# First cross attention of a two-layer perceiver: 16 rounds of one head become 32 rounds of half a head's keys, with a running maximum

## The reference, cut to what matters

```python
N_HEADS = 16
bs, width, length = qkv.shape            # 1, 256, 512
ch = width // N_HEADS                     # 16
q = qkv.reshape(bs * N_HEADS, ch, length)
k = v = y.reshape(bs * N_HEADS, ch, -1)   # 16 heads, 16 channels, 8192 keys
scale = 1.0 / math.sqrt(math.sqrt(ch))
weight = jnp.einsum('bct,bcs->bts', q * scale, k * scale)
weight = jax.nn.softmax(weight.astype(jnp.float32), axis=-1)
a = jnp.einsum('bts,bcs->bct', weight, v)
```

## Time and profile before

| | |
|---|---|
| median of 3 runs | 1461.67 us (1461.64 to 1463.94) |
| the profiled execution, its time | 1462.05 us |
| its span, first to last instruction | 1460.3 us |
| PE busy over the span | 1395.1 us, 96% |
| DVE busy | 1158.6 us, 79% |
| ACT busy | 938.6 us, 64% |
| POOL busy | 107.5 us, 7% |
| the first cross attention in the span | 0 to 705.8 us |

### The profile page before, as it was taken

How to read it: one execution, slowest core, us unless ns; L and a number is a source line. 1 busy time by engine, 2 the same in 40 slices (tenths; PEclk the granted TensorE clock), 3 DMA queues, 4 the chain that set the end, 5 groups by cost and what they waited for, 6 DMA issues and landing times. The chain is left out here.

```text
span 1460.3 us, 27039 instructions
## 1 busy us (share of the span) xinstructions
PE 1395.1 (96%) x10692; PEld 848.0 (58%) x10692; DVE 1158.6 (79%) x1638; ACT 938.6 (64%) x1738; POOL 107.5 (7%) x98
## 2 busy tenths in 40 slices
PE   3999999999999999999899999999989889999998
PEld 1533333333333333333357899999978664567998
DVE  5999999999999999993577666666658546887665
ACT  1188888888888888889275445455534541785553
POOL 8301111111110111100000000000000000000000
PEclk9999999999999999999999999999999999999999
DMA  7334465544544444455203654554446523104540
GB/s 171 85 71 101 115 163 143 143 132 101 115 88 113 91 96 100 115 74 73 87 1 136 266 191 172 186 200 174 173 151 267 230 81 151 65 2 159 190 177 38
DMA packets 36191, 189.34 MB, mean 130 GB/s; under 512 B 8904, under 2 KB 9328, under 8 KB 24048
## 3 DMA queue, kind: packets, MB, share of 16 engines
q1 hardware_dynamic: 35888, 187.62, 42.9%
q10 hardware_dynamic: 192, 0.20, 0.1%
HBM read 163.23 MB, written 21.27 MB: 126 GB/s over the span
## 5 line engine op out<-in xcount | busy, mean ns | idle before, releaser
L451 DVE TENSOR_REDUCE pm<-bank 128x1 f32<-128x1024 f32 x512 | 621.6, 1222 | 18.6 <-PE bank L525 15.7
L505 ACT ACTIVATE probs<-bank 128x512 f32<-128x512 f32 x1024 | 553.6, 598 | 122.5 <-PE bank L540 60.3
L525 PE MATMUL bank<-kst,qst 50*128 50x512 f32 x1024 | 371.7, 460 | 27.2 <-DMA qst<-qsplit 20.5
L540 PE MATMUL bank<-qst,kst 50*128 50x512 f32 x1024 | 363.0, 445 | 2.0 <-DVE pm L451 0.8
L553 PE MATMUL bank<-probs,vext 128*32 128x256 f32 x3840 | 306.5, 391 | 0.0
L540 PEld LDWEIGHTS bank<-qst,kst 50*128 50x128 f32 x1024 | 150.0, 184 | 213.7 <-ACT probs L505 195.5
L1200 PE MATMUL bank<-e_xhi,e_hi 128*128 128x256 f32 (+1 forms) x784 | 222.3, 284 | 3.2 <-DVE e_lo L1135 2.6
L1200 PE MATMUL bank<-e_xhi,e_lo 128*128 128x256 f32 (+1 forms) x784 | 222.2, 283 | 0.0
L1200 PE MATMUL bank<-e_xlo,e_hi 128*128 128x256 f32 (+1 forms) x784 | 222.1, 283 | 0.0
L525 PEld LDWEIGHTS bank<-kst,qst 50*128 50x128 f32 x1024 | 148.2, 189 | 46.1 <-DVE pm L451 23.8
L553 PEld LDWEIGHTS bank<-probs,vext 128*32 128x32 f32 x3840 | 75.6, 108 | 170.8 <-issue 94.2
(11 more groups left out here) (218 smaller groups left out, 1496.9 us busy)
## 6 DMA issues: line engine op xcount, KB each, us to landing
raw<-wall SPq DMA_DIRECT2D x34, 1536.0 KB, 6.6
kst<-kscratch SPq DMA_DIRECT2D x192, 128.0 KB, 4.3
raw<-wall SPq DMA_DIRECT2D x10, 2304.0 KB, 8.6
kscratch<-ksplit SPq DMA_DIRECT2D x15, 1024.0 KB, 4.5
kraw<-ctx_rows SPq DMA_DIRECT2D x16, 512.0 KB, 4.3
vraw<-ctx_vt SPq DMA_DIRECT2D x16, 512.0 KB, 4.7
ctxT<-ctxT SPq DMA_DIRECT2D x8, 1024.0 KB, 12.2
nat<-ctx_chunks SPq DMA_DIRECT2D x6, 1024.0 KB, 21.5
```

The lines of the kernel that those rows point to most:

```text
L451: nc.vector.tensor_reduce(pm[:, h % 2, r % 4, r // 4:r // 4 + 1], bank[:, 2 * (r % 2):2 * (r % 2) + 2, :], AX.XY, ALU.max).then_inc(pre_re ...
L505: nc.scalar.activation(probs[:, (XT * h + n) % PR, :], bank[:, bank_of(h, n), :], ACT.Exp, scale=XSCALE).then_inc(probs_ready, 1)
L525: ins = nc.tensor.matmul(bank[:, 2 * (r % 2) + j, :], qst[64 * j:64 * j + KR, h, tt * P:tt * P + P], kst[64 * j:64 * j + KR, h % 2, c * 51 ...
L540: nc.tensor.matmul(bank[:, bank_of(h, n), :], kst[64 * j:64 * j + KR, h % 2, m * P:m * P + P], qst[64 * j:64 * j + KR, h, :], start=True, ...
```

## The change

A head's 8192 keys are taken in two halves, and the loop's unit is now half a head (`k`, 32 of them; h, half = divmod(k, 2)), with 16 rounds, 32 scores and 8 value groups each. The first half is exponentiated against its own maximum, the second against the maximum over the whole head (a running maximum in `pm`). Two more rows of `qst` (50 and 51) hold the second half's negated maximum; in `kst`, rows 48 and 49 hold ones for the first half of the keys and zeros for the second, rows 50 and 51 hold ones. These rows are written from a small tile `marks` with four transfers instead of POOL's memsets.

The maxima go through memory: one transfer writes `nblocks` to `nscratch`, SP waits for it, and two read it back into `qst`. This is now done for every half head.

The first half's sums have to be multiplied by the exponential of the difference of the maxima: POOL takes the difference (`mdiff`), ACT the exponential (`weight`), SP sends it through memory to all partitions (`store_weight`, `spread_weight`), POOL multiplies (`weigh`) and adds the halves (`sum_o`). ACT copies bank 6 to `osb` twice a head, after the seventh exponential of a unit (`n == 6`).

The first value group of a unit is now whole (`pv_group`) and stands at the end of round 11. `FIRST_BUSY` goes from 18 to 4: idle-filling matmuls begin in round 4 of the first unit's 16 rounds, formerly in round 18 of 32. The order of SP's transfers and of POOL's work is rewritten. In the last unit, PE sums head 15's two halves in bank 2 and 3 with matmuls.

```diff
-KR = 3 * XC + 2
+KR = 3 * XC
+NS = 2
+XN = NS * XH
-XP = XT // 2
-XG = XT // 4
+XST = XT // NS
+XP = XST // 2
+XG = XST // 4
-LAST_BANKS = [0, 1, 4, 5, 7]
+LAST_BANKS = [0, 1, 7, 4, 5]
-FIRST_BUSY = 18
+FIRST_BUSY = 4
...
+            def stack_negmax(k):
+
+                sp.wait_ge(negmax_turned, k + 1)
+                sp.dma_start(nscratch[k], nblocks[:, k % 2, :]).then_inc(negmax_stacked, 16)
+                sp.wait_ge(negmax_stacked, 64 + 48 * k + 16)
+                for j in range(2):
+                    row = 64 * j + KR + 2 * (k % NS)
+                    sp.dma_start(qst[row:row + 2, k // NS, :].rearrange("k (t q c) -> k t q c", t=4, q=4).bitcast(F32),
+                                 nscratch[k].rearrange("(q k t) c -> k t q c", q=4, k=8)[0:2]).then_inc(negmax_stacked, 16)
+
+            def store_weight(h):
+
+                sp.wait_ge(weight_ready, h + 1)
+                sp.dma_start(wscratch[h].rearrange("(p t) -> p t", t=4), weight[:, :]).then_inc(weight_moved, 16)
+
+            def spread_weight(h):
+
+                sp.wait_ge(weight_moved, 32 * h + 16)
+                if h > 0:
+                    sp.wait_ge(weighted, h)
+                sp.dma_start(weights[:, :, :].rearrange("p c t -> p (c t)"), wscratch[h].partition_broadcast(P)).then_inc(weight_moved, 16)
...
-            def stack_negmax(h):
-
-                sp.wait_ge(negmax_turned, h + 1)
-                for j in range(2):
-                    for q in range(4):
-                        to = qst[64 * j + 32:64 * j + 34, h, :].rearrange("k (t q c) -> k t q c", t=4, q=4)[:, :, q, :]
-                        sp.dma_start(to.bitcast(F32), nblocks[32 * q:32 * q + 8, h % 2, :]).then_inc(negmax_stacked, 16)
...
+            def weigh(h):
+
+                pool.wait_ge(weight_moved, 32 * h + 32)
+                pool.wait_ge(o_copied, NS * h + 1)
+                first = osb[:, 0, :].rearrange("p (t c) -> p c t", t=4)
+                nc.gpsimd.tensor_tensor(first, first, weights[:, :, :], ALU.mult).then_inc(weighted, 1)
+
+            def sum_o(h):
+
+                pool.wait_ge(weighted, h + 1)
+                pool.wait_ge(o_copied, NS * h + 2)
+                nc.gpsimd.tensor_tensor(osb[:, 1 + h % 2, :], osb[:, 1 + h % 2, :], osb[:, 0, :], ALU.add).then_inc(o_summed, 1)
...
-                    if n == 5 and h > 0:
-                        copy_o(h - 1)
-            copy_o(XH - 1)
+                    if n == 6 and k > 0:
+                        copy_o(k - 1)
+                    if n == 26 and k % NS == 0:
+                        act.wait_ge(apart, k // NS + 1)
+                        if k // NS > 0:
+                            act.wait_ge(weight_moved, 32 * (k // NS))
+                        nc.scalar.activation(weight[:, :], mdiff[:, k // NS % 2, :], ACT.Exp, scale=XSCALE).then_inc(weight_ready, 1)
+            copy_o(XN - 1)
...
-            for h in range(XH - 1):
+            for k in range(XN - 1):
                 for i in range(XP):
                     for e in range(2):
-                        late_score(h, 2 * i + e)
-                        pre(h + 1, i, 1 - e)
-                        if e == 0 and i == FIRST_V + 1:
-                            late_values(h, FIRST_V)
-                    if h == 0 and i < LAGP:
-                        first_busy(3, 1)
-                    elif h == 0 and i < LAGP + 1 + PVLAG:
+                        late_score(k, 2 * i + e)
+                        pre(k + 1, i, 1 - e)
+                    if k == 0 and i < LAGP:
+                        first_busy(3)
+                    elif k == 0 and i < FIRST_V:
                         for n in range(2):
-                            nc.tensor.matmul(bank[:, 6, :], qst[0:KR, 1, 0:P], kst[0:KR, 1, 0:512], start=True, stop=True)
-                    if i != FIRST_V:
-                        late_values(h, i)
+                            nc.tensor.matmul(bank[:, 6, :], qst[0:KR, 0, 0:P], kst[0:KR, 0, 0:512], start=True, stop=True)
+                    if i == FIRST_V + 1:
+                        pv_group(k, 0)
+                    elif i != FIRST_V:
+                        late_values(k, i)
```

More of the change, by code:

```diff
@@ L357, in _ @@
             load_nd(XH - 2)
-            sp.wait_ge(scores, XT * (XH - 1))
+            sp.wait_ge(scores, XST * (XN - 2))
             for h in range(XHA):
@@ L363, in _ @@
         def _(pool):
-            for j in range(2):
-                nc.gpsimd.memset(qst[64 * j + 32:64 * j + 34, 0, :].bitcast(F32), 0.0).then_inc(const_set, 1)
-            pool.wait_ge(const_set, 2)
             nc.gpsimd.memset(ident[:, :], 0.0).then_inc(g.ident_ready, 1)
@@ L372, in _ @@
             pool.wait_ge(g.ident_ready, 2)
-            for j in range(2):
-                nc.gpsimd.memset(kst[64 * j + 32:64 * j + 34, 0, 0:XK // 2].bitcast(F32), 1.0).then_inc(const_set, 1)
-            pool.wait_ge(const_set, 4)
             def split(h):
@@ L428, in _ @@
+            weigh(XH - 1)
         @block.vector
@@ L543, in pv, with values_ready @@
-            def pv(h, q, half):
+                        pe.wait_ge(probs_ready, XST * k + n + 1 - len(LAST_BANKS))
+                elif k > 0 or n >= 3:
+                    pe.wait_ge(probs_ready, XST * k + n - 2)
+                nc.tensor.matmul(bank[:, bank_of(k, n), :], kst[64 * j:64 * j + rows, h % 2, m * P:m * P + P],
+                                 qst[64 * j:64 * j + rows, h, :], start=True, stop=True).then_inc(scores, 1)
+            def values_ready(k, q):
+                pe.wait_ge(probs_ready, XST * k + 4 * q + 4)
+                if q == 0:
+                    if k % NS == 0:
+                        pe.wait_ge(v_ready, k // NS + 1)
+                    if k > 0:
+                        pe.wait_ge(o_copied, k)
```

264 lines of the change are left out of this document (143 added, 121 removed).

## The result

The changed kernel takes 1467.97 us (median of 6 runs, 1466.2 to 1471.51), the kernel before 1461.66 (6 runs, 1460.74 to 1463.94): ratio 1.0042, 95% interval 1.0032 to 1.0053. It is 6.3 us slower, where 4.3 us faster was forecast. The profiled execution took 1468.59 us.

A forecast was written before the change was run, and what follows sets the result against it. PE's rounds bound the steady pace (1.233 us), with a stall per head and a chain of reads at the end. -18.1 + 19.7 + 0.65 - 6.5 = -4.3 us gives 1457.4 us, range 1450 to 1466.

The forecast's parts named there:

- the price of the spread in front of the last reads: Stage's end: the weight's 256 KB spread ahead of the nine last reads delays them by about 1.0 us.
- the unit of 19.93 us: Steady loop: each half head takes 16 rounds of 1.233 us plus a stall of 0.20.
- First unit, -18.1: Start of the stage: pre-scores stand alone for 16 rounds, no longer 32, at 1.13 us each; 18.1 us off.
- Rounds beside scores and the stall: Loop: 496 rounds for 480, +19.7 us; PE's stall of 0.20 us 31 times for 0.37 15 times, +0.65.
- the walk: Step-by-step reckoning of PE and ACT from round 10 to 12: step of 2.67 us, stall 0.20.
- Rival (b): Rounds 10 to 12: the stall stays at 0.37 us a unit, 5.3 us more, 1463 us; chance 0.12.
- Rival (a): Rounds 10 to 12: the first group's stall goes entirely, 6.2 us less, 1451 us; chance 0.12.
- The maxima's way: From DVE's maximum through memory to PE's eighth round: 5.8 us, 2.0 before the deadline, so it costs nothing.
- Both are in time by over 3 us: SP's queue: work ahead of each half's maxima is due over 3 us early, so it does not delay them.
- Rival (c): Score of n = 0, every unit: maxima late at the eighth round; 0.3 late 1467, 1.1 late 1491 us; chance 0.13.
- The end, -6.5: After DVE's last maximum: the nine reads, not ACT, set the stage's end at +43.7 us, formerly +50.2.
- rival (d): Stage's end: last reads run faster or start sooner, ACT's chain ends it at +36, 7.5 less, 1450 us; chance 0.06.

The follow-up runs named there:

- e12: Kernel before with only the maxima's way changed: through memory in three transfers in place of eight direct ones; ratio 1.0005.
- e3: Changed kernel without head 15's weight: its store, its 256 KB spread and POOL's product left out; 1459.91 us, single run.
- e7: Changed kernel with the end's transfers reordered: most oscratch reads issued earlier, the weight's spread last, DVE summing nd[0] first; 1454.41 us, single run.
- e1: Changed kernel with ACT's copy of bank 6 one exponential earlier, behind a unit's sixth; 1469.68 us, ratio 1.0057.
- e2: Changed kernel with the copy of bank 6 behind the sixth exponential and the first value group again in two halves; 1468.78 us, ratio 1.0043.
- e4: Changed kernel with three of the six early reads of oscratch issued one iteration of SP's loop earlier; 1467.11 us, single run.
- e8: Changed kernel with the copy of bank 6 behind the fifth exponential (last unit as changed) and half a value group in every round; 1468.48 us, single run.
- e15: Changed kernel with the second half's scores over 50 rows in place of 52, leaving that half's maximum out; 1466.28 us, single run.
- e13: Kernel before with pre-scores over 34 rows in place of 50, leaving products out of the maxima; 1909.39 us, single run.
- e14: Kernel before with pre-scores over 48 rows in place of 50, leaving two of the third product's channels out of the maxima; 1463.01 us, single run.
- e10: Kernel before with pre-scores over 32 rows in place of 50, leaving the third product out of the maxima; 2743.42 us, single run.

## Why the prediction was wrong

The forecast was 10.6 us too low, and it is the sum's parts, not one of them. In the profile: 4.5 us at the last reduction, 3.1 from there to the stage's end, 3.1 behind the stage. The step that failed most clearly is the price of the spread in front of the last reads, 1.0 in the sum and 4.1 in the traces; the unit of 19.93 us is the second.

- *First unit, -18.1*: right. The second unit was to start near 40.8 and starts at 40.91.
- *Rounds beside scores and the stall*: mis-sized by 2.7 us over 30 units. A unit is 20.02 us and not 19.93, and it is 20.05 without the first, whose 19.03 nobody had forecast. The step from round 10 to 12 is 2.75 where "2.67 on PE" was forecast, a stall of 0.28 for 0.20, by the hand-over of 0.15 us for which the walk had 0.04; the pitch of 1.233 is 1.240 in most units and 1.236 on average. Rival (b) had the stall whole, at 0.37, and the mechanism was not that; as a unit's time it is the nearer one all the same (20.10 by it), by luck, since the longer round makes up for the shorter stall. Rival (a) is out.
- *A sum on two footings*: 0.6 us. 32 x 1.233 + 0.37 is 39.83, and a head measured 39.79; I added up the first while starting from the second.
- *The maxima's way*: right in 30 units (5.6 us for 5.8, e12 at 1.0005). The page "DMA: Bandwidth & Descriptors" of the Trainium skill (section "Anatomy of one DMA — SWDGE (gpsimd) path") gives about 2.0 us of fixed cost a DMA, for transfers that GpSimd issues; these were issued by SyncE, and 24 of 32 such writes took 1.42 to 1.44 us, the others 1.7 to 4.8. "Both are in time by over 3 us" looked at SP's queue and not at what was in flight: behind six reads of 256 KB the last unit's write took 4.8 us. Rival (c)'s mechanism happened once, for 1.1 us.
- *The end, -6.5*: PE was done at +31 and the reads were issued at +8.1, both as forecast, and DVE's part of 13.4 is exact. The failed step is "about 1.0 for the spread's own 256 KB in front": it cost 4.1 us, since the first read landed 8.4 us after its issue where it had landed after 4.3 in before and 4.2 in e3. So the end saved 3.4 us, not 6.5. Where the prediction has DVE idle "some 7 us more before the sum of `nd[0]`", it contradicts its own sum, by which that sum starts 6 us sooner after the last maximum; DVE waited 10.47 and 8.27 us, in before 13.38 and 8.38. The mechanism of rival (d), reads that start sooner and an end at +36, came true only when e7 brought it about.
- *"What follows it is untouched"*: the instructions are, the time is not. Rows of the view by stretches, of after:

```profile
693.00:710.00 17.00, 0.65 (x3) 0.14 (x2) 13.38 (x10) 0.25 (x1) 0.00 (x0) 0.61 0.04 5
...
1202.00:1208.00 6.00, 4.86 (x17) 2.71 (x16) 2.02 (x9) 1.46 (x4) 0.00 (x0) 0.50 1.03 415
```

  (us, busy PE, PEld, DVE, ACT, POOL, granted clock, DMA share, GB/s.) PE now idles from 693.4 to 709.8, and the clock is at 0.5 from 696.80 to 713.87 (before: 704.26 to 711.09); that cost nothing, the next large matmuls start 6.3 us after the stage's end and before 6.6. But at 1201.97 to 1208.80 there is a stretch at half clock that before does not have, behind an idle of PE of 2.2 us at a seam of stages. DVE's timeline around it, the same two instructions in before and then in after:

```profile
1199.21 1.00 DVE L161 TENSOR_SCALAR xn<-X,mv,rstd 128x512 f32<-128x512 f32 x2
1205.58 0.69 DVE L854 TENSOR_TENSOR a_rot<-bank,bias_row 128x512 f32<-128x512 f32 x1 [5.37 <-PE bank L738]
...
1203.46 1.00 DVE L164 TENSOR_SCALAR xn<-X,mv,rstd 128x512 f32<-128x512 f32 x2
1212.12 0.69 DVE L918 TENSOR_TENSOR a_rot<-bank,bias_row 128x512 f32<-128x512 f32 x1 [7.66 <-PE bank L802]
```

  From the first to the second it is 6.37 us in before and 8.66 in after: 2.3 of the 3.1 us lie in this stretch. Nothing ties it to the change: before has the same idle of 2.2 us there at full clock, and so have e1, e2, e4, e8 and e15, whose instructions behind the stage are after's and whose PE idles as long at its end. They took 754.6 to 756.3 us from the stage's end to the span's end, before 754.5, after 757.6. The 0.8 us outside the stretch is within what these five show against before (0.2 to 1.8). So 2.3 us of the miss were bad luck in the profiled execution; how often such a stretch falls into the six timed runs of either kernel is not known.

As to theories: mine after the result was that the loss is the spread and the six early reads. e3 and e7 bore out the end; e4 bore out the six reads, but for 1.1 us alone, and in e1 and e15 they cost nothing. The larger part of the loop's loss, 0.1 us in each unit, is the hand-over and the pitch, of which only the first has a cause.

## What to carry to other kernels

Where a change shortens the work in front of a fixed chain of transfers, the chain is the new end: price it from the first issue to the last landing, and move the transfers first. Count what is in flight, not only what is queued, before a small transfer with a deadline; and a spread of one row to all partitions is no transfer of its bytes. A price that is paid at each seam (a bank's hand-over, 0.28 us) is paid twice as often when the unit is halved, while the gain, half a head less at the start, comes once. And compare a part that the change does not touch in several executions before giving its difference a cause.

## What the runs showed of the hardware

- A 16 KB write to memory from 128 partitions took 1.42 to 1.44 us from issue to the wait behind it in 24 of 32 units of after, 1.7 to 3.6 in seven, and 4.8 behind six 256 KB reads. Over the ten kernels of half heads that have this write once, a transfer of the instruction queue q8 was under way in 58 of the 75 writes above 1.6 us and in 15 of the other 245; this was seen, not tested.
- A spread of 256 KB from 2 KB in memory lands in 3.8 us (median of 16; 7.1 with nine reads behind it) and delays nine reads behind it by 4.1 us (after against before and e3).
- With pre-scores over 34 rows instead of 50 (e13), TensorE's records show no full clock before 1113.56 us; with 48 (e14) it was there from 45.1, as in before from 45.49. Beside 50-row matmuls, 32-row ones did not run side by side (e10), 34-row ones did (e13).
- A round of the same instructions has two paces, 1.227 and 1.240 us, which hold through a unit.
- After 2.2 us without a matmul at the same place of the program, the clock fell to 0.5 for 6.83 us in one execution (after) and stayed full in six others (before, e1, e2, e4, e8, e15); the stretch cost 2.3 us.
